# One layer's gather block: ScalarE's order dealt anew, own rows at the opening, the last band of slots in two pieces

## The reference, cut to what matters

```python
h = (x_flat @ W_gat).reshape(M, HEADS, NUM_EXPERTS)     # M = 32768 nodes, 4 heads, 4 values
src = concatenate([edge_index[0], loops]); dst = concatenate([edge_index[1], loops])
e = leaky_relu(a_src[src] + a_dst[dst], 0.2)
ee = exp(e - segment_max(e, dst)[dst])
alpha = ee / (segment_sum(ee, dst)[dst] + 1e-16)
agg = segment_sum(h[src] * alpha[:, :, None], dst) + b_gat
scores = layernorm(agg).reshape(M, HEADS, NUM_EXPERTS).mean(1)     # top 2 of 4 experts
out = sum over experts of gate * (gelu(x @ W1[e] + b1[e]) @ W2[e] + b2[e])
```

## Time and profile before

| | |
|---|---|
| median of 3 runs (lowest, highest) | 2439.89 us (2437.56, 2441.52) |
| profiled execution: own time, span | 2444.8 us, 2443.0 us |
| busy over the span | PE 1922.1 us, DVE 1568.1, ACT 1038.6, POOL 719.5 |
| gather block | from 2194.0 us (first gather) to 2393.8 us (DVE's last copy) |
| granted TensorE clock, whole span | 0.867 of full speed |

### The profile page before, as it was taken

The page is one execution under the profiler, slowest core; times in us unless marked ns, Lnnn a source line. Parts: engine busy times, 40 slices in busy tenths (PEclk is TensorE's granted clock), DMA queues, the critical chain, the costliest instruction groups (busy, mean ns, idle before and its releaser), DMA issues. The chain is left out here.

```text
span 2443.0 us, 27067 instructions
## 1 busy us (share of the span) xinstructions
PE 1922.1 (79%) x9142; PEld 904.9 (37%) x9142; DVE 1568.1 (64%) x3609; ACT 1038.6 (43%) x1724; POOL 719.5 (29%) x703
## 2 busy tenths in 40 slices
PE   2976887798699766679967888878878887978594
PEld 1323422332243234456643222222322324864264
DVE  4787777768786775546726575665566554634657
ACT  1433142233304215545533667656656662214355
POOL 3302600630170041024441322332322322127750
PEclk8987998889789877879987999999988986768797
DMA  7002100300120000021001111101011000014100
GB/s 197 1 21 68 35 2 25 77 17 20 39 62 1 22 6 1 1 102 21 14 29 52 42 31 41 42 16 40 29 31 36 3 5 15 1 37 79 10 7 35
DMA packets 55446, 80.18 MB, mean 33 GB/s; under 512 B 17249, under 2 KB 28504, under 8 KB 55073
## 3 DMA queue, kind: packets, MB, share of 16 engines
q1 hardware_dynamic: 44806, 69.14, 9.6%
q10 hardware_dynamic: 6426, 7.99, 1.5%
q0 software_dynamic: 4096, 1.58, 1.3%
HBM read 50.13 MB, written 24.68 MB: 31 GB/s over the span
## 5 line engine op out<-in xcount | busy, mean ns | idle before, releaser
L2475 DVE TENSOR_REDUCE f_half_max<-f_ring 128x1 f32<-128x512 f32 x512 | 334.3, 685 | 274.9 <-PE f_ring L2138 274.1
L2358 ACT ACTIVATE f_probs<-f_ST 128x512 f32<-128x512 f32 x512 | 292.9, 597 | 213.5 <-PE f_ST L2165 209.3
L2138 PE MATMUL f_ring<-f_stacks 96*128 96x512 bf16 x512 | 207.1, 405 | 52.3 <-DVE f_half_max L2475 25.5
L809 DVE TENSOR_REDUCE att_half_max<-att_ring 128x1 f32<-128x512 f32 x256 | 163.0, 685 | 86.7 <-PE att_ring L691 85.4
L2165 PE MATMUL f_ST<-f_stacks 99*128 99x512 bf16 x512 | 204.0, 404 | 11.8 <-ACT f_probs L2358 11.8
L792 ACT ACTIVATE att_probs<-att_ST 128x1024 f32<-128x1024 f32 x128 | 129.3, 1023 | 155.1 <-PE att_ST L716 154.9
L2182 PE MATMUL f_O<-f_probs,f_v_ext 128*32 128x512 f32 x1024 | 153.3, 674 | 0.1
L3197 POOL DMA_INDIRECT ti_row<-features,slot_from x128 | 128.3, 1002 | 56.8 <-issue 56.8
L2138 PEld LDWEIGHTS f_ring<-f_stacks 96*128 96x128 bf16 x512 | 50.7, 99 | 247.3 <-DVE f_half_max L2475 149.8
L734 PE MATMUL att_O<-att_probs,v_ext 128*64 128x512 f32 x512 | 133.9, 650 | 6.6 <-DVE att_den L828 6.6
L716 PE MATMUL att_ST<-stacks 96*128 96x512 bf16 (+1 forms) x512 | 137.6, 397 | 0.0
(11 more groups left out here) (594 smaller groups left out, 3678.8 us busy)
## 6 DMA issues: line engine op xcount, KB each, us to landing
f_stacks<-f_parts SPq DMA_DIRECT2D x192, 64.0 KB, 2.2
parts_dram<-l_parts SPq DMA_DIRECT2D x8, 768.0 KB, 3.6
stacks<-parts_dram SPq DMA_DIRECT2D x24, 256.0 KB, 9.7
stacks<-parts_dram ACTq DMA_DIRECT2D x24, 256.0 KB, 10.6
f_parts<-f_parts SPq DMA_DIRECT2D x8, 768.0 KB, 3.5
es_raw<-L_ffn_edge_index SPq DMA_DIRECT2D x8, 512.0 KB, 4.7
bm_mix<-mix SPq DMA_DIRECT2D x8, 512.0 KB, 10.1
xn_cm<-x SPq DMA_DIRECT2D x4, 512.0 KB, 3.4
```

Of the source, the lines that this page charges most:

```text
L809: nc.vector.tensor_reduce(half_max[:, h % 2, t, n:n + 1], ring[:, i % RING], AX.X, ALU.max, negate=True).then_inc(reduced, 1)
L2138: nc.tensor.matmul(ring[:, i % RING], f.stacks[0:STACK, 0, at, t * P:(t + 1) * P], f.stacks[0:STACK, 1, at, n * BANK:(n + 1) * BANK], star ...
L2358: nc.scalar.activation(f.probs[:, s % PROBS, n * BANK:(n + 1) * BANK], ST[:, i % HALVES], ACT.Exp).then_inc(probs_ready, 1)
L2475: nc.vector.tensor_reduce(f.half_max[:, h % 2, t, n:n + 1], ring[:, i % RING], AX.X, ALU.max, negate=True).then_inc(reduced, 1)
```

## The change

- Slots are worked in five pieces instead of four bands: `PIECES = ((0, 0, 32), (1, 32, 64), (2, 64, 96), (3, 96, 116), (3, 116, 128))`, that is (band, first slot, end). Bands 0 to 2 are as before, band 3 is worked as 20 and then 12 slots, both into the same 8 tokens. Each piece has its own semaphore of the gather, its pack and its exponents; the tiles keep their size and are used up to the piece's number of slots.
- ACT's order is `TO_START = 5`, `TO_PACK = (10, 19, 27, 31, 32)`, `TO_BEND = (12, 21, 29, 32, 32)`: half-runs 0 to 4, the own rows' exponential, 5 to 9, pack 0, 10 and 11, exponents 0, 12 to 18, pack 1, 19 and 20, exponents 1, 21 to 26, pack 2, 27 and 28, exponents 2, 29 and 30, pack 3, 31, exponents 3, pack 4, exponents 4.
- DVE makes the own rows' values right after L3382, ahead of all bands, and `refill.place` comes after piece 0.

```diff
-    TO_PACK, TO_BEND = (8, 15, 22, 29), (9, 16, 23, 30)
+    TO_START, TO_PACK, TO_BEND = 5, (10, 19, 27, 31, 32), (12, 21, 29, 32, 32)
...
+PIECES = ((0, 0, 32), (1, 32, 64), (2, 64, 96), (3, 96, 116), (3, 116, 128))
...
-        for g in range(BANDS):
-            for j in range(g * SLOTS, (g + 1) * SLOTS):
+        for i, (_, lo, hi) in enumerate(PIECES):
+            for j in range(lo, hi):
...
-        self.nc.scalar.activation(self.p[:], self.z[:], ACT.Exp).then_inc(exped, 1)
+        self.nc.scalar.activation(self.flat(self.p, hi - lo), self.flat(self.z, hi - lo), ACT.Exp).then_inc(exped, 1)
...
+    def flat(x, slots):
+        return x.rearrange("p h t j -> p (h t) j")[:, :, 0:slots]
...
-            at = 0
-            for g in range(BANDS):
-                bend(at, experts.TO_PACK[g])
-                t.pack(act, g, gathered, packed, banded)
-                bend(experts.TO_PACK[g], experts.TO_BEND[g])
-                t.exponents(act, g, shifted, exped)
-                if g == 1:
-                    act.wait_ge(starting, 1)
-                    nc.scalar.activation(n[:, 1:3], n[:, 1:3], ACT.Exp).then_inc(started, 1)
-                at = experts.TO_BEND[g]
+            at = experts.TO_START
+            bend(0, at)
+            act.wait_ge(starting, 1)
+            nc.scalar.activation(n[:, 1:3], n[:, 1:3], ACT.Exp).then_inc(started, 1)
+            for i in range(len(PIECES)):
+                bend(at, experts.TO_PACK[i])
+                t.pack(act, i, gathered, packed, banded)
+                bend(experts.TO_PACK[i], experts.TO_BEND[i])
+                t.exponents(act, i, shifted, exped)
+                at = experts.TO_BEND[i]
...
-            for g in range(2):
-                t.band(dve, link, g, packed, shifted, exped, banded)
-            refill.place(dve, link, spread)
...
-            for g in range(2, BANDS):
-                t.band(dve, link, g, packed, shifted, exped, banded)
+            for i in range(len(PIECES)):
+                t.band(dve, link, i, packed, shifted, exped, banded)
+                if i == 0:
+                    refill.place(dve, link, spread)
```

More of the change, by code:

```diff
@@ L3193, in gather @@
     def gather(self, pool, gathered):
-        for g in range(BANDS):
-            for j in range(g * SLOTS, (g + 1) * SLOTS):
+        for i, (_, lo, hi) in enumerate(PIECES):
+            for j in range(lo, hi):
                 self.nc.gpsimd.indirect_dma_start(self.row[:, j, :], None, self.k.features, bass.IndirectOffsetOnAxis(
-                    ap=self.k.slot_from[:, j:j + 1], axis=0)).then_inc(gathered[g], 16)
-        for g in range(BANDS):
-            pool.wait_ge(gathered[g], 16 * SLOTS)
@@ L3202, in pack @@
[L3202 to L3207, removed]
+                    ap=self.k.slot_from[:, j:j + 1], axis=0)).then_inc(gathered[i], 16)
+        for i, (_, lo, hi) in enumerate(PIECES):
+            pool.wait_ge(gathered[i], 16 * (hi - lo))
+    def pack(self, act, i, gathered, packed, banded):
+        _, lo, hi = PIECES[i]
+        act.wait_ge(gathered[i], 16 * (hi - lo))
+        if i >= 2:
+            act.wait_ge(banded, i - 1)
+        self.nc.scalar.copy(self.packed[:, i % 2, :, 0:hi - lo], self.row[:, lo:hi].rearrange(
@@ L3208, in pack, with exponents @@
             "p j f -> p f j")).then_inc(packed, 1)
-    def exponents(self, act, g, shifted, exped):
-        act.wait_ge(shifted, g + 1)
+    def exponents(self, act, i, shifted, exped):
+        _, lo, hi = PIECES[i]
+        act.wait_ge(shifted, i + 1)
         self.nc.scalar.activation(self.n[:, 1], self.n[:, 1], ACT.Exp).then_inc(exped, 1)
-        self.nc.scalar.activation(self.p[:], self.z[:], ACT.Exp).then_inc(exped, 1)
-    def band(self, dve, link, g, packed, shifted, exped, banded):
-        nc, k, e, n, hot, z, p, y = self.nc, self.k, self.e, self.n, self.hot, self.z, self.p, self.y
-        tile, row = k.slot_tile[:, g * SLOTS:(g + 1) * SLOTS], self.packed[:, g % 2]
+        self.nc.scalar.activation(self.flat(self.p, hi - lo), self.flat(self.z, hi - lo), ACT.Exp).then_inc(exped, 1)
@@ L3218, in band @@
+    @staticmethod
+    def flat(x, slots):
+        return x.rearrange("p h t j -> p (h t) j")[:, :, 0:slots]
+    def band(self, dve, link, i, packed, shifted, exped, banded):
+        nc, k, e, n = self.nc, self.k, self.e, self.n
+        g, lo, hi = PIECES[i]
+        slots = hi - lo
+        hot, z, p, y = self.hot[:, :, 0:slots], *(x[:, :, :, 0:slots] for x in (self.z, self.p, self.y))
+        tile, row = k.slot_tile[:, lo:hi], self.packed[:, i % 2, :, 0:slots]
         tiles = slice(g * BAND, (g + 1) * BAND)
-        wide, whole = [P, BAND, SLOTS], [P, GH, BAND, SLOTS]
@@ L3220, in band @@
-        link(nc.vector.tensor_tensor(hot[:], k.tiles[:, tiles].unsqueeze(2).broadcast_to(wide),
+        wide, whole = [P, BAND, slots], [P, GH, BAND, slots]
+        link(nc.vector.tensor_tensor(hot, k.tiles[:, tiles].unsqueeze(2).broadcast_to(wide),
                                      tile.unsqueeze(1).broadcast_to(wide), ALU.is_equal))
-        link(nc.vector.tensor_scalar(hot[:], hot[:], -NEG, NEG, ALU.mult, ALU.add))
+        link(nc.vector.tensor_scalar(hot, hot, -NEG, NEG, ALU.mult, ALU.add))
@@ L3224, in band @@
         top, shift, a_dst, den = (x[:, :, tiles] for x in (k.top, k.shift, e.a_dst, k.den))
-        best, change, total, part, own = (n[:, i] for i in range(5))
+        best, change, total, part, own = (n[:, x] for x in range(5))
         link(nc.vector.tensor_copy(own, a_dst))
@@ L3231, in over_slots @@
         def over_slots(x):
[L3232 to L3236, removed]
+            return flat(x).unsqueeze(2).broadcast_to([P, GH * BAND, slots])
+        z3, p3, y3 = (self.flat(x, slots) for x in (self.z, self.p, self.y))
+        dve.wait_ge(packed, i + 1)
+        link(nc.vector.tensor_tensor(z, hot.unsqueeze(1).broadcast_to(whole),
                                      row[:, 0:GH].unsqueeze(2).broadcast_to(whole), ALU.add))
@@ L3247, in band @@
         nc.vector.tensor_tensor(z3, z3, over_slots(best), ALU.subtract).then_inc(shifted, 1)
-        dve.wait_ge(exped, 2 * (g + 1))
+        dve.wait_ge(exped, 2 * (i + 1))
         link(nc.vector.tensor_reduce(flat(total), p3, AX.X, ALU.add))
@@ L3254, in band @@
             value = row[:, GH:GH + GH * GE].rearrange("p (h v) j -> p v h j", v=GE)[:, v]
-            m = nc.vector.tensor_tensor(y[:], p[:], value.unsqueeze(2).broadcast_to(whole), ALU.mult)
+            m = nc.vector.tensor_tensor(y, p, value.unsqueeze(2).broadcast_to(whole), ALU.mult)
             link(m)
@@ L3263, in band @@
                 last.then_inc(banded, 1)
-                dve.wait_ge(banded, g + 1)
+                dve.wait_ge(banded, i + 1)
 class Refill:
@@ L3338, in take_in_slots @@
              "stored", "spread", "parted", "hidden_ready", "hidden_off", "made", "carried",
-             *(f"gathered_{g}" for g in range(BANDS)), pool_dma=True))
+             *(f"gathered_{i}" for i in range(len(PIECES))), pool_dma=True))
         @block.tensor
```

## The result

Over nine runs of each, the changed kernel takes 2424.38 us (median; 2419.9 to 2434.74) and the kernel before 2438.36 us (2433.55 to 2448.39): a ratio of 0.9947, with a 95% interval of 0.9931 to 0.9963, so some 12.9 us less (9 to 17; the two medians lie 13.98 us apart). It is faster, inside the range, and near the 12.3 us forecast.

The account below looks back on a forecast made before the run. The gather block was bounded by ACT's lateness plus a whole band, ending with DVE's copies at 2393.8 us. Ending at 2381.5 (2368.6 + 12.4 + 0.5) saves 12.3 us, giving 2427.6 us against the median; range 2423 to 2432.

Parts of the forecast that it names:

- ACT's lateness plus a whole band: End of the gather block before the change: ACT behind with half-runs after its 25.1 us wait, then a band of 22.2 us.
- The opening: Before pack 0: 12.6 us of DVE's own-rows work falls into a wait and costs nothing; PE loses 1 us.
- The middle: Pieces 0 to 2: PE keeps 4.45 us per half-run, packs 1 and 2 on time, exponents 2 with 2.6 us to spare.
- The last band: Band 3 as 20 and 12 slots: DVE's pieces take 16.35 and 12.4 us, exponents 3 start 1.4 us late, end at 2381.5.
- The bound of 2.0 us for exactly half the clock: Last band: the most that exponents 3 could be late if PE made output 31's 16 products at half clock.
- The sum: Whole kernel: block end from 2393.8 to 2381.5, 12.3 us less, so 2427.6 us against the median; forecast's chance 0.57.
- Exponents 3 on time: Rival, piece 3: PE keeps full clock or starts its products sooner; 1.4 us more, 13.7 saved, 2426.2 us; chance 0.15.
- The gather: Rival, piece 4: slot 127's rows packed later than 2368.6 set the end; 9.3 us saved, 2430.6 us; chance 0.14.
- Cut tiles: Rival, last two pieces: cut tiles cost as much as whole ones, 15.0 us back, 2442.6 us; chance 0.03.
- Half-runs late: Rival, copy of output 31: if it ends at 2368 instead of 2355.6, nothing is left, 2439.9 us; chance 0.05.
- a slower TensorE: Rival, half-runs before exponents 3: PE at 1.2 GHz; with ten such half-runs 22 us later, 2462 us; chance 0.03.
- The rule on the shared port pair: Gathers beside DVE: two-input DVE and GpSimd SBUF reads exclude each other; delays at most 0.6 us seen, 1.5 us taken.

Follow-up runs that it names:

- run 31: Part of half-run 31, ACT's last half-run, not a follow-up run; moved in the changed kernel ahead of pack 3 (ratio 0.9933) or to ACT's end (0.9936).

## Why the prediction was right

**What bounds the block.** The stall of 25.1 us was the cause of ACT's lateness: taking it away without the split gives 6 us (the own rows early), and leaving it makes the split harmful (+6.1 us). That the end was "ACT's lateness plus a whole band" is borne out by both.

**The opening.** The own rows' 12.6 us went into DVE's wait for pack 0, which is still 11.9 us long. ACT waited from 2217.78 to 2222.41, 4.6 us including its table load instead of the 6.7 forecast: its half-runs were 1.5 us later than forecast, and `starting` came 0.6 us earlier. PE's first products, the hidden layers of the first three half-runs, began 0.2 us later against the gathers and took 8.2 us instead of 6.9, at a granted clock of 0.57 instead of 0.73 from 2190 to 2205. This lies ahead of anything the change touches.

**The middle.** PE kept 4.45 us for a half-run up to pack 2 and a granted clock of 1.00 from 2205 to 2341. ACT had its table for exponents 0 at 2250.22, 0.3 us before DVE's `shifted`, not 1.1, and DVE waited no longer for exponents 0 and 1 than before (1.24 us). Pack 1 came 1.6 us later than forecast: its last gather started 1.0 us later, by the long one beside band 0, and its rows came 3.93 us after that start instead of 3.36. Pack 2 came 1.5 us later, by this and a second long gather (1.92 us, slot 68). By piece 3 it was 0.5 us: I had put 0.6 us more on slots 96 to 115 than they took, 0.2 of it a slip (2317.55 + 1.16 + 0.30 + 19 x 1.25 + 2.2 is 2345.0, not 2345.2), and the rows came 2.88 us after slot 115's start. So the start of piece 3 came out near the forecast by misses that cancel.

**The last band.** Forecast and measured, with 2.06 added to the forecast: rows of piece 3 at 2350.7 and 2351.2; the 16 products 3.8 and 3.40 us after a stand of 10 and 8.15; exponents 3 late by 1.4 and 0.93 (1.33 in the second profile); piece 3 through at 2369.9 and 2369.95; pack 4 ready at 2368.1 and 2368.4; last copy at 2383.6 and 2383.50. The two small misses, a later start and a shorter lateness, cancel, so the match to 0.1 us is luck; the match to 1 us is not. Moving half-run 31 in two ways took the lateness away, so its cause is shown. The bound of 2.0 us for exactly half the clock should read 1.7 (16 products in 4.1 us, made at 2355.3, table loaded by 2357.2); the longest that the runs show for them is 3.79 us.

**The sum.** 12.3 against 12.4 us in the block; in the whole time 12.9 (9 to 17). The 2427.6 us were counted from a median of three runs; from the 2438.36 of nine the same sum gives 2426.1, against 2424.38. The sentence that the last stage has the same instructions was wrong by one: the table load of the earlier trace rows is gone, because the loop now ends in an Exp. DVE waits 0.48 us there instead of 0.76, so it is worth 0.3 us. The stage was 1.1 us shorter in the two profiles, but over all of them the stretch behind the block lies between 48.1 and 50.6 us, and the rest is scatter.

**The rivals.** Exponents 3 on time would have given 0.9 us, not 1.4. The gather was 2.3 us from setting the end, and in the cut of 18 and 14 it does. Cut tiles cost by their elements. Half-runs late, and a slower TensorE: the clock stayed up. What was argued for these two, that the new order leans on PE more than the old one, is not borne out for a PE 15 per cent slower: both kernels lost nearly the same. The changed kernel has its slack in the waits for the gather, and this much used it up; the old one, behind ACT's stall, had none there.

**Gathers beside DVE, and the table load.** The rule on the shared port pair was weighed by delays of at most 0.6 us. In the changed kernel one gather took 1.96 us, 1.02 more than the usual, and started 0.09 us after L3255, a two-input instruction of 1.23 us:

```profile
2246.84 1.96 POOL L3198 DMA_INDIRECT ti_row<-features,slot_from  x1 [0.30 <-issue]
```

```profile
2246.75 1.23 DVE L3255 TENSOR_TENSOR ti_z<-ti_z,ti_new 128x1024 f32<-128x1024 f32 x1
```

That fits what the Trainium skill (SBUF — State Buffer, section "SBUF: two separate sides") has, that the later one is held for the whole instruction. The 14 traces, read gather by gather, show it more sharply. Behind the first three of a block, 221 gathers took over 1.1 us. Every one of them had started 0.06 us or more into a two-input instruction (TENSOR_TENSOR) of DVE, and ended 0.80 to 0.84 us after that instruction's end, whatever its length. In the row above: 2246.75 + 1.23 + 0.82 = 2248.80. None of the 75 that started at least 0.3 us before the end of a MAX8 or a TENSOR_REDUCE, up to 4.1 us before it, took over 0.95 us. So DVE's bands are the cause, and what counts is which instruction a gather meets and when. Six gathers that started in the first 0.03 us of a wide two-input instruction weren't held at all, and here DVE, not the gather, lost some 0.05 us (1.28 instead of 1.23):

```profile
2243.09 0.94 POOL L3198 DMA_INDIRECT ti_row<-features,slot_from  x1 [0.30 <-issue]
```

```profile
2243.06 1.28 DVE L3246 TENSOR_TENSOR ti_z<-ti_hot,ti_packed 128x1024 f32<-128x1024 f32 x1 [11.92 <-ACT ti_packed L3209]
```

The Trainium skill (same section) gives the ports for the whole instruction to whichever starts first; these rows don't bear that out the other way round, as DVE wasn't held for the gather's 0.94 us. So a few hundredths of a microsecond decide between no delay and one of 1.02 us. The table load stayed 1.28 us.

## What to carry to other kernels

Find out of a wait whether it is for data or for an engine that is behind with other work: the same split of the last tile cost 6 us while ACT was behind and gave 6 us once it waited for the data. Move small dependent work into the longest wait ahead of it before tuning the order around it. Cut the last tile so that the last piece's data are ready just as the engine finishes the piece ahead. Compare small changes in the length of the stage they touch, which here repeated within 0.1 us in two pairs of profiles where the whole time scattered by 7 us and more; and look even there for what is luck, as the held gathers were 1.2 to 1.6 us of a difference of 2.5.

## What the runs showed of the hardware

- An indirect gather of 128 rows was issued each 1.25 us (0.94 us and a gap of 0.30). Beside DVE's bands single ones were held by 0.2 to 1.0 us, and the last of 128 started 5.8 to 9.3 us later than with DVE idle (164.9 to 168.4 us against 159.1). Each that took over 1.1 us had started in a TENSOR_TENSOR and ended 0.8 us after it; beside MAX8 and TENSOR_REDUCE none was held.
- The length of PE's stand alone didn't tell the pace behind it. Behind stands of 3.32 and 3.42 us in the two profiles of the changed kernel its next four products took 1.98 us, nearly the full pace; behind 3.44 us in the run with 18 and 14 slots they took 3.54, and behind 6.1 us in the kernel before 3.78.

```profile
2327.28 1.98 PE L2746 MATMUL gm_ps<-xn_cm,x 128*128 128x512 f32 x4 [3.32 <-ACT turned L2810]
```

- A strided copy of 128x480 took 1.31 us and one of 128x288 0.83, against 2.10 for 128x768: nearly in proportion, with little fixed cost (1.4 and 0.9 were forecast).
